# Order of the last chunk's first row, the ends of the branch arms, and two outer products on GpSimd

## The reference

```
k, v, q = x W_k, x W_v, x W_q ;  k = k / (|k| + 1e-6) per block of 8
S = tanh(S + (v - S k) outer k) ;  out = S q, times silu(S q)
```

## Time and profile before

| | us |
|---|---|
| median of 3 runs | 1154.36 |
| lowest, highest | 1153.38, 1154.7 |
| the profiled execution | 1153.3 |
| its span in the trace | 1151.5 |
| busy: PE, DVE, ACT, POOL | 1096.3, 956.9, 596.8, 513.7 |
| mean granted clock of PE | 0.978 |

### The profile page before, as it was taken

One profiled execution on the slowest core, in us unless ns is written; L12 is line 12 of the kernel. 1 busy time (PEld: TensorE's weight loads), 2 busy tenths in 40 slices (PEclk: granted clock), 3 DMA queues, 4 the chain that ended last, 5 costly groups with the idle time before them and its releaser, 6 DMA issues.

```text
span 1151.5 us, 16583 instructions
## 1 busy us (share of the span) xinstructions
PE 1096.3 (95%) x5821; PEld 850.0 (74%) x5821; DVE 956.9 (83%) x1384; ACT 596.8 (52%) x1009; POOL 513.7 (45%) x424
## 2 busy tenths in 40 slices
PE   9999999999999999999999999999999999998376
PEld 5666666678787777788778787877887787786264
DVE  4788888872045998999899899989988998998896
ACT  2345555563445346555745564466457356653534
POOL 1477666774343235333324432443442234336741
PEclk9999999999999999999999999999999999997787
DMA  7256655524532431423234043313423331420001
GB/s 270 95 177 230 219 208 205 202 92 128 165 92 74 128 110 38 128 73 128 74 110 147 18 128 91 117 50 107 120 80 93 91 126 36 129 74 19 0 1 39
DMA packets 45115, 127.02 MB, mean 110 GB/s; under 512 B 4352, under 2 KB 21504, under 8 KB 43136
## 3 DMA queue, kind: packets, MB, share of 16 engines
q1 hardware_dynamic: 43904, 114.20, 31.2%
q10 hardware_dynamic: 1152, 12.07, 2.8%
HBM read 117.86 MB, written 19.92 MB: 120 GB/s over the span
## 4 chain that ended last, share of the span: by engine, by line
PE 76%; DVE 11%; POOL 7%; issue 3%; ACT 2%; POOLq 0%; DVEq 0%; ACTq 0%
PE lower L1218 45%; PE bank L1218 18%; PE lower L440 5%; PE lower L572 2%; POOL state L748 2%; POOL rgn L757 2%; PE bank L1207 1%; DVE y L847 1%; DVE y L852 1%; PE bank L487 1%; POOL a_lo L1952 1%; POOL mixw L1997 1%; PE lower L526 1%; DVE tmp L2180 1%; PE lower L530 1%
## 5 line engine op out<-in xcount | busy, mean ns | idle before, releaser
L1952 POOL TENSOR_TENSOR a_lo<-whole,a_hi 128x512 fp32r<-128x512 f32 x128 | 181.9, 1439 | 268.3 <-ACT a_hi L1565 197.1
L1218 PE MATMUL lower<-b_hi,ring 128*128 128x512 f32 x512 | 193.6, 396 | 1.4 <-ACT a_hi L1565 1.4
L1218 PE MATMUL lower<-b_lo,ring 128*128 128x512 f32 x512 | 190.6, 390 | 1.7 <-POOL b_lo L1952 1.7
L1218 PE MATMUL lower<-a_hi,ring 128*128 128x512 f32 x496 | 186.4, 394 | 1.7 <-issue 1.7
L1218 PE MATMUL lower<-a_lo,ring 128*128 128x512 f32 x496 | 184.2, 390 | 0.2 <-POOL a_lo L1952 0.2
L1952 POOL TENSOR_TENSOR b_lo<-whole,b_hi 128x512 fp32r<-128x512 f32 x64 | 93.9, 1474 | 145.3 <-ACT b_hi L1565 145.3
L1548 ACT ACTIVATE S<-S 128x1024 f32<-128x1024 f32 x56 | 58.6, 1059 | 183.2 <-DVE S L2188 183.2
L1564 ACT ACTIVATE whole<-lower,hs 128x512 f32<-128x512 f32 x126 | 86.3, 685 | 76.9 <-PE lower L1218 71.7
L1218 PEld LDWEIGHTS lower<-b_hi,ring 128*128 128x128 f32 x512 | 96.2, 188 | 21.9 <-issue 1.8
L1218 PEld LDWEIGHTS lower<-b_lo,ring 128*128 128x128 f32 x512 | 96.0, 188 | 22.0 <-POOL b_lo L1952 2.3
L440 PE MATMUL lower<-wa,xT 128*128 128x512 f32 x240 | 109.3, 599 | 1.4 <-DVE turned L817 1.4
(11 more groups left out here) (295 smaller groups left out, 2394.2 us busy)
## 6 DMA issues: line engine op xcount, KB each, us to landing
ring<-ffn_copy_dram SPq DMA_DIRECT2D x128, 512.0 KB, 3.6
look<-ffn_dram ACTq DMA_DIRECT2D x6, 1879.0 KB, 6.9
ffn_copy_dram<-ffn_dram SPq DMA_DIRECT2D x4, 2112.0 KB, 10.6
rope<-rope_dram SPq DMA_DIRECT2D x8, 512.0 KB, 7.9
xtok<-x_dram SPq DMA_DIRECT2D x8, 512.0 KB, 4.6
x1in<-x_dram SPq DMA_DIRECT2D x8, 512.0 KB, 4.9
x1res<-x_dram SPq DMA_DIRECT2D x8, 512.0 KB, 3.3
xT<-xT_dram SPq DMA_DIRECT2D x7, 512.0 KB, 8.5
```

The lines of the kernel that those rows point to most:

```text
L1218: ins = nc.tensor.matmul(out, a, b, start=(first and n == 0), stop=(last and n == len(pairs) - 1))
L1952: nc.gpsimd.tensor_tensor(lo[:, m, :], t["whole"][:, m % 4, :], hi[:, m, :].bitcast(F32), ALU.subtract).then_inc(lo_done, 1)
```

## The change

- The last chunk's `down` is taken out of `body` on TensorE and becomes `last_down(b)`, with waits for the last two parts of the input only where they are read; row 3 stands behind the turn of row 0. ScalarE's tanh of step (3, 0) goes behind gelu 15.
- Row 0: on VectorE `ffn_row(0)` goes ahead of the second half of `update(3, 1)`, which is cut in `update_sum` and `update_state` with rows 1 to 3 and the first `guess_of` between them. On GpSimd `mix_weights` is cut in four pairs, one ahead of the first `x2_root`. On ScalarE `query_row(0)` and `x2_rows` of rows 1 to 3 go ahead of the tanh of (3, 1).
- `last_root` and `last_mix` keep their bodies (`last_root` L2530, `last_mix` L2536) and are called inside both arms.
- The outer products of steps 2 and 3, second half, are GpSimd operations (`outer_product`, 128 x 1024, all in SBUF), with `state_delta` and `state_added` on VectorE around them; semaphore values follow tables. `read_q` of a second half waits for the tanh and no longer for VectorE's product; `read_q(2, 1)` and `added_mean(1)` go ahead of `read_q(3, 0)`; `gate_rows(front)` goes behind `state_added(2)`.
- `busy_while_waiting`: eight f32 matmuls whose results are not used, between pair 1 and pair 2 on TensorE. On ScalarE `add_squares` goes ahead of `mix_gates(1, 1)`.

The diff without the moved bodies of `last_root` and `last_mix`, 12 columns of indentation taken off:

```diff
@@ -1092,6 +1092,15 @@
     return bank[b][:, 0:DIM]
+READS = {(0, 0): 1, (0, 1): 2, (1, 0): 3, (1, 1): 4, (2, 0): 6, (2, 1): 7, (3, 0): 9}
+OUTERS = {1: 5, 2: 8}
+TIMES_K = {(0, 0): 1, (0, 1): 2, (1, 0): 3, (1, 1): 4, (2, 0): 6, (2, 1): 7}
+DELTAS = {1: 5, 2: 8}
+def last_outer(t):
+    return t["S"][:, 0:HALF]
 NORM_STEPS = 13
...
             rows = slice(b * P, b * P + P)
-            last = isinstance(c, int) and c == LAST
-            out = bank[b][:, 0:DIM] if last else bank[b // 2][:, (b % 2) * DIM:(b % 2) * DIM + DIM]
+            out = bank[b // 2][:, (b % 2) * DIM:(b % 2) * DIM + DIM]
...
-            if last:
-                ins.then_inc(fin_w3, 1)
-            elif b % 2:
+            if b % 2:
                 ins.then_inc(w3_ps, 1)
+    def last_down(b):
+        rows, steps = slice(b * P, b * P + P), LAST * SPLITS + 3 * KH
+        if narrow_w:
+            pairs = [(x[:, k, rows], w3r[:, k, :]) for k in range(KH) for x in (t["a_hi"], t["a_lo"])]
+            pe.wait_ge(hi_done, steps - 1)
+            pe.wait_ge(lo_done, steps - 1)
+            product(bank[b][:, 0:DIM], pairs[:-2], last=False)
+            pe.wait_ge(hi_done, steps)
+            product(bank[b][:, 0:DIM], pairs[-2:-1], first=False, last=False)
+            pe.wait_ge(lo_done, steps)
+            ins = product(bank[b][:, 0:DIM], pairs[-1:], first=False)
+        else:
+            pe.wait_ge(act_done, LAST * 2 * KH + 2 * KH)
+            ins = product(bank[b][:, 0:DIM],
+                          [(t["a"][:, k, rows], weight(COL_W3, k, DIM, 0, DIM)) for k in range(KH)])
+        ins.then_inc(fin_w3, 1)
@@ -1383,7 +1437,7 @@
                 hidden(i, 1, m)
             if more:
                 up(i + 1, range(2))
-            down(i)
+                down(i)
...
+        def busy_while_waiting():
+            pe.wait_ge(pair_sig, 2)
+            for _ in range(8):
+                nc.tensor.matmul(pair_banks(2)[1][:, 0:DIM], ident[:], wk[:, 0, :], start=True, stop=True)
...
+        for b in range(3):
+            last_down(b)
         turn_row(0)
+        last_down(3)
         key_value_row(0)
         query_row(0)
...
+        busy_while_waiting()
         turn_pair(2, 0)
         pair_products(2, 0)
@@ -1683,8 +1747,9 @@
                 if n == 2:
                     scan_tanh(c, 0, 0)
                     scan_tanh(c, 0, 1)
-                if n in (5, 7, 9, 14):
-                    half = (5, 7, 0, 9, 14).index(n)
+                at = (5, 7, 9, 14 if more else 2 * KH - 1)
+                if n in at:
+                    half = (0, 1, 3, 4)[at.index(n)]
                     scan_tanh(c, 1 + half // 2, half % 2)
             if n == KH - 1:
...
             if n:
-                act.wait_ge(fin_readq, 7 if (n, hf) == (BATCH - 1, 1) else 2 * (n - 1) + hf + 1)
+                act.wait_ge(fin_readq, READS[n - 1, hf])
             cols = slice(hf * half_cols, (hf + 1) * half_cols)
             nc.scalar.activation(S7[:, cols], before7[:, cols], ACT.Tanh).then_inc(fin_post, 1)
@@ -1829,15 +1894,15 @@
             nc.scalar.activation(pair_result(t, g)[:, 2 * n:2 * n + 2, :], pair_banks(g)[2][:].rearrange("p (b d) -> p b d", b=2),
                                  ACT.Tanh, scale=0.5).then_inc(pair_sig, 1)
-        scan_tanh(d, BATCH - 1, 1)
         x2_rows(0, range(1))
         turned_row(0)
         act.wait_ge(out_done, 16 * (LAST - 1))
         key_value_row(0)
+        query_row(0)
         x2_rows(1, range(1, BATCH))
+        scan_tanh(d, BATCH - 1, 1)
         for b in range(1, BATCH):
             turned_row(b)
-        query_row(0)
         key_value_row(1)
         act.wait_ge(sq_done, (d + 1) * 2 * BATCH)
         sqf = Sq[:].rearrange("p b d -> p (b d)")
...
         key_acts(1, 1)
         add_rows(1, x3, range(0, 2), fin_x3, 1)
+        add_squares(1, x3, range(0, 2))
         mix_gates(1, 1)
-        add_squares(1, x3, range(0, 2))
         state_tanh(3, 1)
         act.wait_ge(fin_rs, 2)
...
             pow_and_shift(rows, t["rstd2"], t["shift2"], t["mv2"][:, rows, 1], t["mv2"][:, rows, 0],
                           added_steps, n + 1, rs2)
-        def mix_weights():
+        def mix_weights(w):
             pool.wait_ge(prep, 6)
             pool.wait_ge(w12_ps, CHUNKS * KH)
+            src, by = ((wk, mu_k), (wk, nu_k), (wr, mu_r), (wr, nu_r))[w]
             for k in range(KD):
-                for w, (src, by) in enumerate(((wk, mu_k), (wk, nu_k), (wr, mu_r), (wr, nu_r))):
-                    nc.gpsimd.tensor_scalar(t["mixw"][:, k, w, :], src[:, k, :], by[:, k:k + 1], None,
-                                            ALU.mult).then_inc(mixw_done, 1)
+                nc.gpsimd.tensor_scalar(t["mixw"][:, k, w, :], src[:, k, :], by[:, k:k + 1], None,
+                                        ALU.mult).then_inc(mixw_done, 1)
         def key_root(n, rows):
...
-            if s == BATCH - 1:
+            if s and (s == BATCH - 1 or hf):
                 pool.wait_ge(fin_post, 2 * s + hf + 1)
             else:
-                pool.wait_ge(fin_times_k, 2 * s + hf + 1)
+                pool.wait_ge(fin_times_k, TIMES_K[s, hf])
             if s:
                 pool.wait_ge(fin_sq, 2 * (s - 1) + hf + 1)
             nc.gpsimd.tensor_tensor(last_buffers(t, hf)[0], st, along_j(q), ALU.mult).then_inc(fin_readq, 1)
+        def outer_product(s):
+            k = half_blocks(t, s + 1, 1)[0]
+            pool.wait_ge(fin_times_k, DELTAS[s])
+            if s == 2:
+                pool.wait_ge(fin_pre, 2 * s + 2)
+            nc.gpsimd.tensor_tensor(last_outer(t), along_i(t["delta"][:, 0:HALF, :]), along_j(k),
+                                    ALU.mult).then_inc(fin_readq, 1)
...
         every, front, back = slice(0, BATCH), slice(0, 2), slice(2, BATCH)
-        mix_weights()
+        mix_weights(0)
         x2_root(0, slice(0, 1))
+        mix_weights(1)
+        mix_weights(2)
         x2_root(1, slice(1, BATCH))
         key_root(0, slice(0, 1))
+        mix_weights(3)
         key_root(1, slice(1, 2))
         added_mean(0, every)
@@ -2067,10 +2144,12 @@
         read_q(0, 1)
         read_q(1, 0)
         read_q(1, 1)
+        outer_product(1)
         read_q(2, 0)
+        read_q(2, 1)
+        outer_product(2)
+        added_mean(1, front)
         read_q(3, 0)
-        added_mean(1, front)
-        read_q(2, 1)
         added_root(1, front, t["rstd3"], t["shift3"])
         pool.wait_ge(ve4, LAST)
...
         start()
     schedule(pool, body)
     finish()
+    last_root(pool)
...
             x1_low(i + 1)
-        if has_scan:
+        if has_scan and not more:
+            read_out(c, 2, 0, scan)
+            update(c, 3, 0)
+            read_out(c, 2, 1, scan)
+        elif has_scan:
             scan_step(c, 2)
             scan.end()
...
+        def state_delta(s):
+            k, v, _, st, _, w = last_parts(s + 1, 1)
+            dl = t["delta"][:, 0:HALF, :]
+            dve.wait_ge(fin_post, 2 * s + 2)
+            nc.vector.tensor_tensor(w, st, along_j(k), ALU.mult).then_inc(fin_times_k, 1)
+            dve.wait_ge(fin_times_k, TIMES_K[s, 1])
+            if s == 2:
+                dve.wait_ge(fin_readq, OUTERS[1])
+            fin.done(nc.vector.tensor_reduce(dl, w, AX_X, ALU.add))
+            fin.wait()
+            nc.vector.tensor_tensor(dl, v, dl, ALU.subtract).then_inc(fin_times_k, 1)
+        def state_added(s):
+            dve.wait_ge(fin_readq, OUTERS[s])
+            _, _, _, st, _, w = last_parts(s + 1, 1)
+            nc.vector.tensor_tensor(w, st, last_outer(t), ALU.add).then_inc(fin_pre, 1)
         def sq_cols(s, hf):
...
-            dve.wait_ge(fin_readq, {(2, 1): 7, (3, 0): 6}.get((s, hf), 2 * s + hf + 1))
+            dve.wait_ge(fin_readq, READS[s, hf])
             nc.vector.tensor_reduce(sq_cols(s, hf), last_buffers(t, hf)[0], AX_X, ALU.add).then_inc(fin_sq, 1)
...
         row_moments(fin, t["mv2"], slice(0, 1), ve2)
+        update_sum(d, 3, 1)
         for b in range(1, BATCH):
             ffn_row(b)
         row_moments(fin, t["mv2"], slice(1, BATCH), ve2)
+        guess_of(slice(0, 1))
+        update_state(3, 1)
+        scan.end()
         earlier_x3(0)
-        guess_of(slice(0, 1))
         earlier_x3(1)
...
         next_state(1, 0)
-        next_state(1, 1)
+        state_delta(1)
         read_sums(1)
+        state_added(1)
         next_state(2, 0)
+        state_delta(2)
+        read_sum(2, 0)
         mixed_pair(0, 0)
+        state_added(2)
         gate_rows(front, 2, 1)
-        read_sum(2, 0)
-        next_state(2, 1)
         mixed_pair(1, 1)
         read_sum(2, 1)
...
     schedule(dve, body)
-    return finish()
...
+    last_mix(dve, finish())
...
 block = ctx.enter_context(nc.Block())
@@ -2600,18 +2688,16 @@
     with pool.Else():
         attention_ends(pool, end.body)
         gpsimd_program(pool, False, end)
-    last_root(pool)
 @block.vector
 def _(dve):
     end = attention_vector(dve)
     flag = wide_words(dve)
     with dve.If(flag < 1):
```

(36 more changed lines are left out.)

27 lines of the change are left out of this document (1 added, 26 removed).

## The result

The changed kernel takes 1148.2 us (median of 5 runs, 1147.44 to 1148.24) where the kernel before takes 1153.94 on the same chip (1153.38 to 1154.7, 5 runs): the ratio is 0.9949, 95% interval 0.9938 to 0.996. Two later sets of five runs gave 0.9945 and 0.9943. The profiled execution took 1148.24 us, its span is 1146.3 (before 1151.5), so 5.2 us are to be found in the trace.

What follows compares the result with a forecast made beforehand. VectorE was taken to bound the last scan's steps, then a chain of small products after 1124. The terms -0.95 (to the gates' products) and -1.24 (end) sum to -2.2, giving 1152.2 us; 8-in-10 range 1149.8 to 1155.2.

Steps and rivals of the forecast that it cites:

- 5: end inside the arm: VectorE's `last_mix` starts when its operands are there, with no branch in between: -1.24 us, bounds 0 and -1.3.
- part 4: TensorE before pair 2's turn: idle some 3 us, so the eight idle matmuls take 5.3 to 7.0 us, earning nothing.
- Parts 1 and 2: Last `down` reordered, row 0 first: VectorE takes row 0 6.1 us earlier, `scaled_keys(1)` starts 3.75 us earlier.
- The row of the forecast: Earlier trace: VectorE's addition beside a `mixw` product took 1.38 us, 0.16 over normal; the sum goes by it.
- the lock on `mixw`: Skill page's rule: row additions and `update_sum` wait for `mixw`, about 0.8 us apiece; the front gives some 2 us less.
- Part 3: Outer products on GpSimd at 2.35 us: gate of rows 0 and 1 2.0 later, shift at 1121.6, -1.35.
- The front gain is kept: `state_delta` is not blocked and the eight matmuls find the clock up: 6.1 us at most, 1149.8; chance 0.22.
- Slower: GpSimd's outer product costs over 3.45 us; at 4.7 it is +2.5, 1156.9; chance 0.11.
- Only the end: Front worth about 2 us less, by lock or lost clock: 0 to -1.2, 1153.2 to 1154.4; chance 0.25.

Runs made afterwards that it cites:

- the front alone: Kernel before with only the last `down` reordered and row 0 first on all engines: 1150.57 us, ratio 0.997.
- ends: Kernel before with only `last_mix` and `last_root` inside the arms: 1152.99 us against 1154.49, ratio 0.9988.

## Why the prediction was wrong

The sum has two terms, -0.95 up to the end of the gates' products of rows 0 and 1, and -1.24 behind it. The trace has -4.01 (1130.59 for 1134.60) and -1.26 (`last_mix` 5.27 earlier in all). The second was right. The first missed by 3.06 us:

| Step | Forecast | Measured |
|---|---|---|
| 2: first `guess_of` | 1054.55 | 1054.30 |
| 2: `first_state` | 1065.2 | 1065.78 |
| 2: `scaled_keys(1)` | 1073.1 | 1073.31 |
| 3: outer product on GpSimd | 2.35 | 1.96, 1.95 |
| 3: stage from `next_state(1,0)` to `(2,0)` | 12.4 | 11.99 |
| 3: gate of rows 0 and 1 ends | 1116.15 | 1114.98 |
| 3: shift ends | 1121.6 | 1120.35 |
| 4: eight matmuls start, take | 1119.0, 5.3 to 7.0 | 1118.69, 3.62 |
| 4: turn of rows 0 and 1 | 1125.15 | 1122.14 |
| 5: end inside the arm | -1.24 | -1.26 |

**The step that failed is part 4**, "TensorE has then been idle some 3 us", and with it "they earn nothing here". The prediction gives no sum for these 3 us, and the row that it compares, 1124.14 in the earlier trace rows, stands behind 5.53 us of idle time. It had itself put `mixed_pair(0,0)` behind the blocked product and a read sum, and followed this on VectorE; it did not ask who waits for `mixed_pair(0,0)` on TensorE. The gates of pair 1 do. An estimate from its own numbers: the first operation of `mixed_pair(0,0)` ends at 1101.85 + 9.85 + 0.7 = 1112.4, gates of 3.6 to 5.4 us and values of 1.7 follow, to 1117.7 to 1119.5, and the eight start at 1119.0: idle for at most 1.3 us, not 3. Measured was no gap in the first trace and 0.73 or 0.74 in three later ones (eight idle matmuls twice, four once), and the eight took 3.62, later 3.72.

The experiments show it from both sides. With that one call moved forward the gap is back (2.70), the eight take 5.41, and 2.1 us are lost, about 1.7 of them by the clock. Without the eight the turn and keys lose their clock, and 1.3 to 2.0 are lost. In the traces of the kernel without outer products, where the gates are early as well, the eight run just as forecast.

**Parts 1 and 2 were right**, and the front alone gives 3.5 us. The row of the forecast decided well against the lock on `mixw`: with two `mixw` products running from 1051.05 on, VectorE's addition at 1051.18 took 0.61 instead of 0.43, and three others beside a `mixw` product (1045.43, 1049.93, 1052.61) took 0.42 to 0.44. By the rule of the Trainium skill ("SBUF — State Buffer", section "SBUF: two separate sides"), a lock for the whole instruction, it would have waited for the first of them, to about 1051.95. For two tensor products the rule held: `read_q(1,1)` ran to 1095.27, and VectorE's product, started at 1094.52, took 1.84 instead of 1.22 and ended 1.09 behind it, where a full wait would be 1.22.

**Part 3 took too high a price.** 1.96 for 2.35 takes away the waiting in each stage, the gate comes 1.2 us earlier, and the shift with it. This too was needed for the miss: by the forecast's shift the turn could not start before 1122.8, 0.66 later than it did, however fast the eight ran. The forecast saw that the outer products put the gate later (by 2.0 with the front's gain taken in). It did not say that without them the kernel would be better, which the medians show: 1.0 and 1.2 us in the whole change. On their own they are at +0.6, not clear of noise. Why the whole change is better without them is argued, not shown: the shift ends at 1118.83 and 1118.86 for 1120.18 to 1120.58, but both traces are of executions that were no faster.

**The parts add up, nearly.** By ratio to 1154: ends -1.4, front -3.5, outer products +0.9, together -4.0; the changed kernel without the eight has -4.4, and with them -5.9, -6.3 and -6.6 in its three sets. So the eight are worth 1.5 to 2.2 there by ratio, 1.3 to 2.0 by medians. Without outer products the whole has -7.6, ends and front -4.9: the eight, together with `add_squares` ahead of `mix_gates(1,1)`, are worth 2.7, more than in the changed kernel. The two were not tried apart, so that the late gates make the eight pay is true of the changed kernel's order only.

**The rivals.** "The front gain is kept" has the measured time at its full price: 1154.36 - 6.1 is 1148.3. The forecast gave it half of what lay beyond its own sum and wrote 1149.8 for it; half of 6.1 - 2.2 makes 1150.2. One of its two conditions held, the eight found the clock up. The other, that GpSimd's read does not block VectorE, did not (1.84 in both stages); the cheaper outer product stood in for it. Nor did the eight end before the turn was due: they held it by about 0.65 us in the first trace, 0.1 in the second. That the number fits is in part luck. "Slower" was out at 1.96 us, far under its 3.45. "Only the end" needed a front worth 2 us less, and it was worth what was forecast.

The best kernel found is the changed one without its outer products, 1146.5 us, or 1146.34 with five idle matmuls; they are 1.0 to 1.4 us under the change as it was made.

## What to carry to other kernels

When an edit puts a step later on one engine, follow each engine that waits for it, also where the delay looks harmless: here a late input closed a gap on TensorE, and with everything else in this order that was worth 2.1 us. It is no gain in itself, for the kernel with the early input and without the outer products was faster still. A filler (matmuls whose results nobody uses) is priced by what the engine did just ahead of it: at full clock it costs its length, behind a gap it can hold up what it was to speed up. Moving work to an idle engine is to be judged by the order that it forces on the others, for two products moved off the engine that was busiest in this stretch made the kernel slower. And before a trace is used to explain a median, its own time is to be set beside it: here the traces of the best kernel are of executions 1.1 and 1.3 us above its median.

## What the runs showed of the hardware

- On GpSimd a 128x1024 product with both inputs broadcast took 1.96 us, one with one input broadcast 2.35.
- After 0.7 to 1.5 us of idle time TensorE's next sixteen records of 256 columns took 3.72 us (gaps of 0.73, 1.14, 1.40, 1.41); after 1.92, 1.93 and 2.70 they took 5.41. Between, the same gap went both ways: the gates of pair 1 took 5.41 behind 2.07 us in the changed kernel's first trace and behind 2.06 with the outer products alone, and 3.72 behind 2.06 with four idle matmuls. The keys of pair 1 took 5.33 to 5.41 behind 3.03 to 3.49 us and 6.05 to 6.42 behind 4.09 to 4.53 (14 traces).
- The clock can still be up right behind a gap and fall after it: with the outer products alone the four transposes behind 2.68 us took 0.66, as at full clock, and the sixteen records behind them 6.71.
- One program has executions with different clocks in the same place, so a single profile does not tell what such an edit is worth.
- Leaving an arm before the last operations cost VectorE 2.88 and 3.04 us of `issue` in two kernels; it came back as 1.3 to 1.4 us of time, as it lay beside TensorE's last product.
